# A graph network kernel on one Trainium2 core: gathers and scatters wait for the landing of the pair two back

## What is computed

```python
edge_index = jnp.stack([src, dst])
edge_index_t = jnp.stack([src, dst], axis=1)
h = jnp.maximum(_layernorm(x, axis=-1), 0.0)
x = x + _L0_gnn_ref(h, edge_attr_16, edge_index_t, ...)
h = jnp.maximum(_layernorm(x, axis=-1), 0.0)
x = x + _L1_gnn_ref(h, edge_index, edge_weight)

# _L0_gnn_ref: edge_index_t[:, 0] is the node that receives, edge_index_t[:, 1] the neighbour
edge_mats = (bond_features @ W_bond + b_bond).reshape(-1, d, d)
for _ in range(STEPS):                                    # STEPS = 4
    msg = jnp.einsum('eij,ej->ei', edge_mats, h[nbr])
    agg = jax.ops.segment_sum(msg, dst, num_segments=n_atoms)
    h = _gru_cell(agg, h, W_ih, W_hh, b_ih, b_hh)

# _L1_gnn_ref
msgs = x[row] * (deg_inv_sqrt[row] * edge_weight * deg_inv_sqrt[col])[:, None]
out = jax.ops.segment_sum(msgs, col, num_segments=num_nodes)
```

## Time and profile before

| | us |
|---|---|
| median of three runs | 32566.4 |
| lowest, highest | 32561.8, 32571.98 |
| the profiled execution | 32329.01 |
| its span, first to last instruction | 32327.5 |
| POOL busy in the span | 19193.7 (59%) |
| TensorE (PE) busy | 18113.4 (56%) |
| VectorE (DVE) busy | 12316.8 (38%) |
| ScalarE (ACT) busy | 6342.0 (20%) |

### The profile page before, as it was taken

One profiled execution on the slowest core, in us unless ns is written; L12 is line 12 of the kernel. 1 busy time (PEld: TensorE's weight loads), 2 busy tenths in 40 slices (PEclk: granted clock), 3 DMA queues, 4 the chain that ended last, 5 costly groups with the idle time before them and its releaser, 6 DMA issues. The chain is left out here.

```text
span 32327.5 us, 272049 instructions
## 1 busy us (share of the span) xinstructions
PE 18113.4 (56%) x73252; PEld 11303.4 (35%) x73253; DVE 12316.8 (38%) x18995; ACT 6342.0 (20%) x11838; POOL 19193.7 (59%) x19883
## 2 busy tenths in 40 slices
PE   5444444447777757777767777775777773000004
PEld 4222222224444434444434444443444442000003
DVE  7555555533333333333333333333333333111113
ACT  4222222212222212222212222221222221000000
POOL 2444444466666656666656666665666665777772
PEclk5666666678888878888878888887888886555555
DMA  2222222211111111111111111111111111222224
GB/s 87 81 77 77 81 77 77 81 35 29 29 29 29 29 25 29 29 29 28 29 26 27 29 29 29 30 28 25 29 29 30 30 29 36 55 55 55 55 55 123
DMA packets 2423090, 1449.76 MB, mean 45 GB/s; under 512 B 1772221, under 2 KB 2253002, under 8 KB 2404167
## 3 DMA queue, kind: packets, MB, share of 16 engines
q1 hardware_dynamic: 720484, 980.18, 10.0%
q0 software_dynamic: 635936, 335.84, 6.4%
q10 hardware_dynamic: 1066560, 132.51, 2.7%
HBM read 1035.83 MB, written 411.12 MB: 45 GB/s over the span
## 5 line engine op out<-in xcount | busy, mean ns | idle before, releaser
L1112 POOL DMA_INDIRECT h_rows<-h_table,rec x12928 | 12195.4, 943 | 7353.8 <-issue 3880.5
L1298 PE MATMUL outer<-a_masked,h_by_quarter 128*128 128x272 f32 x25856 | 8240.2, 447 | 5227.6 <-DVE h_by_quarter L1158 2359.8
L1298 PEld LDWEIGHTS outer<-a_masked,h_by_quarter 128*128 128x128 f32 x25856 | 5378.2, 216 | 9576.1 <-issue 7355.3
L1266 PE MATMUL msg_psum<-outer_sums,w_bond_blocks 128*128 128x512 f32 x13736 | 7718.0, 652 | 0.0
L1344 ACT COPY outer_sums<-outer 128x544 f32<-128x544 f32 x6464 | 3900.2, 613 | 15272.9 <-PE outer L1298 7098.1
L865 POOL DMA_INDIRECT edges_by_node<-row,place x3125 | 2992.3, 958 | 3188.2 <-DVE row L792 2273.2
L1598 POOL DMA_INDIRECT messages_by_bucket<-ms,ix x3232 | 3418.9, 1058 | 1149.1 <-issue 1124.9
L1150 DVE TENSOR_TENSOR a_masked<-rec,gates 128x4352 f32<-128x4352 f32 x808 | 3782.5, 4681 | 53.1 <-PE outer L1298 31.5
L1266 PEld LDWEIGHTS msg_psum<-outer_sums,w_bond_blocks 128*128 128x128 f32 x13736 | 2921.0, 213 | 923.6 <-issue 260.9
L1167 DVE TENSOR_TENSOR_SCAN scan<-carry_flags,scan,msg_psum 128x512 f32<-128x512 f32 x404 | 517.1, 1280 | 6706.2 <-PE msg_psum L1266 4495.5
L1158 DVE TENSOR_TENSOR h_by_quarter<-h_rows,gates 128x2048 f32<-128x2048 f32 x808 | 1846.0, 2285 | 1824.4 <-DMA h_rows<-h_table,rec 1786.2
(11 more groups left out here) (273 smaller groups left out, 12928.5 us busy)
## 6 DMA issues: line engine op xcount, KB each, us to landing
h_rows<-h_table,rec POOLq DMA_INDIRECT x12928
key_row<-source_keys SPq DMA_DIRECT2D x125, 1600.0 KB
rec<-edges_by_node SPq DMA_DIRECT2D x1010, 168.0 KB
carry_flags<-carry_flags SPq DMA_DIRECT2D x505, 256.0 KB
chunk_sums<-scan_t ACTq DMA_DIRECT2D x1616, 64.0 KB
low_key_row<-source_low_keys SPq DMA_DIRECT2D x126, 800.0 KB
mr<-messages_by_bucket SPq DMA_DIRECT2D x220, 392.0 KB, 3.0
messages_by_bucket<-zeros SPq DMA_DIRECT2D x125, 689.5 KB
```

Of the source, the lines that this page charges most:

```text
L1112: pool.indirect_dma_start(out=hb[r][:, u, :], out_offset=None, in_=ht, in_offset=bass.IndirectOffsetOnAxis(ap=rec[r][:, u, W_DST:W_DST + 1 ...
L1266: last = pe.matmul(pm[:, 0:GW], wb[:, k, :], ts[b][:, k, :], start=(k == 0), stop=(k == K1 - 1))
L1298: last = pe.matmul(pt[g % RING][:, u, 0:KC], hq[j][:, g * GPB + u, :, :].rearrange("p q d -> p (q d)"), am[j][:, g * GPB + u, :, :].rearra ...
```

## The change

POOL's transfers now wait for each other. The four semaphores `s_hg` no longer stand for the four buffers but for the pairs of gathers in turn: pair k of a tile (u = 2k and 2k+1) raises `s_hg[k % 4]`. Ahead of each pair stands a wait for the landing of the pair two back, also across tiles, with a `hold`; the first two pairs of a step's first tile are without it where nothing was issued yet. `spread_h` waits for all four semaphores in place of one.

The 25 scatters of an iteration are cut into eight turns (seven of three, one of four) over four semaphores `s_sc`, and each turn waits for the landing of the turn two back. A new semaphore `s_free` ("rows_free_again"), which POOL raises when it comes to an iteration's second turn, tells ScalarE and VectorE that the other `row` buffer may be written; they wait on it where they waited on `s_sc[b]`. The loop over iterations becomes `pairs_after_first`. No data transfer and no computation is added, taken out or made larger.

```diff
@@ the sort: semaphores
-            s_sc = [sem(f"rows_scattered{b}") for b in range(2)]
+            s_sc = [sem(f"rows_scattered{k}") for k in range(4)]
+            s_free = sem("rows_free_again")
+            TURNS = [(a, a + 3) for a in range(0, J1 - 4, 3)] + [(J1 - 4, J1)]
+            PER = [16 * sum(z - a for a, z in TURNS[k::4]) for k in range(4)]
@@ make_row (ScalarE) and place_stage 0 (VectorE)
-                        act.wait_ge(s_sc[b], i * (16 * J1))
+                        act.wait_ge(s_free, it + 1)
...
-                            dve.wait_ge(s_sc[b], i * (16 * J1))
+                            dve.wait_ge(s_free, it + 1)
@@ the scatters (POOL)
+                    pool.sem_inc(s_free, 2)
                     clear_flags(range(HB // 2))
-                    def scatter(it, b, i):
+                    def scatter(it, b, i, first):
                         pool.wait_ge(s_row, it + 3)
                         pool.wait_ge(s_place, it + 3)
                         hold(pool)
-                        for u in range(J1):
-                            pool.indirect_dma_start(
-                                out=r3, out_offset=bass.IndirectOffsetOnAxis(ap=place[b][:, u:u + 1], axis=0),
-                                in_=row[b][:, u, :], in_offset=None).then_inc(s_sc[b], 16)
-                    pairs(pool, IT1, scatter)
+                        for k, (u0, u1) in enumerate(TURNS):
+                            before = (k - 2) % 4
+                            after = 16 * sum(z - a for a, z in TURNS[before:max(0, k - 1):4])
+                            if not (first and k < 2):
+                                pool.wait_ge(s_sc[before], it * PER[before] + after)
+                                if k == 1:
+                                    pool.sem_inc(s_free, 1)
+                                else:
+                                    hold(pool)
+                            for u in range(u0, u1):
+                                pool.indirect_dma_start(
+                                    out=r3, out_offset=bass.IndirectOffsetOnAxis(ap=place[b][:, u:u + 1], axis=0),
+                                    in_=row[b][:, u, :], in_offset=None).then_inc(s_sc[k % 4], 16)
+                    pairs_after_first(pool, IT1, scatter)
@@ the steps: the gathers (POOL)
-            s_hg = [sem(f"h_gathered{j}") for j in range(RB)]
+            s_hg = [sem(f"h_gathered{k}") for k in range(4)]
+            HPI = 16 * J3 // 4
...
                                     if u in (0, LATER) and past:
                                         pool.wait_ge(s_t, n0 * NB + (j * NB + NB + (HALF // GPB if u else 0)))
                                         hold(pool)
+                                    k = u // 2
+                                    if u % 2 == 0 and (k >= 2 or j or past):
+                                        pool.wait_ge(s_hg[(k - 2) % 4], n0 * HPI + (j * HPI + 32 * ((k + 2) // 4)))
+                                        hold(pool)
                                     pool.indirect_dma_start(
                                         out=hb[r][:, u, :], out_offset=None, in_=ht,
                                         in_offset=bass.IndirectOffsetOnAxis(ap=rec[r][:, u, W_DST:W_DST + 1].bitcast(I32), axis=0)
-                                    ).then_inc(s_hg[r], 16)
+                                    ).then_inc(s_hg[k % 4], 16)
@@ the steps: spread_h (VectorE)
-                            dve.wait_ge(s_hg[r], (s * USES[b] + i) * (16 * J3) + 16 * J3)
+                            for landed in s_hg:
+                                dve.wait_ge(landed, n * HPI + HPI)
                             dve.wait_ge(s_t, n * NB + NB)
```

More of the change, by code:

```diff
@@ L124, in gnn_program @@
     assert T3 * P < BIG and T2 * P < BIG and HB <= P and HB * D <= 7 * 512 and NGR % 2 == 1 and NRUN % 4 == 0
-    assert RB == 2 * GI and GI * HT == TU and CT <= P and GW <= 512
+    assert J3 == 16 and RB == 2 * GI and GI * HT == TU and CT <= P and GW <= 512
     r3 = nc.dram_tensor("edges_by_node", [T3 * P, W3], F32).ap()
@@ L510, in gnn_program @@
             s_row = sem("rows_made")
-            s_sc = [sem(f"rows_scattered{b}") for b in range(2)]
+            s_sc = [sem(f"rows_scattered{k}") for k in range(4)]
+            s_free = sem("rows_free_again")
+            TURNS = [(a, a + 3) for a in range(0, J1 - 4, 3)] + [(J1 - 4, J1)]
+            PER = [16 * sum(z - a for a, z in TURNS[k::4]) for k in range(4)]
+            assert len(TURNS) == 8
             s_v3 = sem("place_chain")
@@ L863, in scatter @@
                         hold(pool)
-                        for u in range(J1):
-                            pool.indirect_dma_start(
-                                out=r3, out_offset=bass.IndirectOffsetOnAxis(ap=place[b][:, u:u + 1], axis=0),
-                                in_=row[b][:, u, :], in_offset=None).then_inc(s_sc[b], 16)
-                    pairs(pool, IT1, scatter)
-                    pool.wait_ge(s_sc[0], 16 * J1 * ((IT1 + 1) // 2))
-                    pool.wait_ge(s_sc[1], 16 * J1 * (IT1 // 2))
+                        for k, (u0, u1) in enumerate(TURNS):
[12 more added lines that the diff above has]
+                    pairs_after_first(pool, IT1, scatter)
+                    for k in range(4):
+                        pool.wait_ge(s_sc[k], PER[k] * IT1)
         lay = ExitStack()
```

## The result

| | before | after |
|---|---|---|
| median of four runs each, same chip, us | 32569.19 | 33981.29 |
| lowest, highest | 32561.8, 32580.95 | 33947.0, 34025.63 |
| span of the profiled execution | 32327.5 | 33970.1 |

The change makes the kernel 4.3% slower: the ratio is 1.0434, with an interval of 1.0416 to 1.0452. That is 1412 us where 133 were forecast, above the whole range. It is also above the rival in which the limit binds (33045 us).

The account below looks back on a forecast made before the run. The prediction took a ring of waits among POOL's gathers, spread_h and TensorE's outer to set the pace. Its terms, 10 + 36 + 87 = 133 us, on 32566.4 gave about 32700 us, 0.4% slower, range 32560 to 32960.

Parts of the forecast that it names:

- the limit binds: Rival, chance 0.12: in the steps one of the last two pairs stalls 0.94 us in 509 tiles; 478 us, 33045 us.
- What bounds the kernel: In a step no engine is full and a ring of waits sets the pace; POOL busy 3043 of 4890 us, TensorE 3606.
- The ring: In the steps POOL's gathers wait for outer (3.6 us each), spread_h for the gathers' landing, and outer for spread_h.
- Whether they are met at once: Steps, ahead of the gather pairs: landing waits met with 0.27 to 0.61 us to spare; 10 us, bounds nothing and 760.
- Waits that are met: Steps, ahead of some 6,460 pairs: waits and holds are covered by the gather's 0.94 us; costed at nothing.
- POOL's second wait at u = 10: Behind the old wait on s_t, POOL's restart passes one more instruction; 509 x 0.07 = 36 us, bounds nothing and 125.
- Four waits in `spread_h`: Two steps, 0.17 us, between the last landing and spread_h in 509 tiles; 87 us, bounds nothing and 194.
- The sort: POOL's turn waits fit into 18.3 us spare per iteration, s_free might come 0.51 us late; nothing taken, 64 us at most.
- The clock: TensorE in the steps: a longer stop can put one more group on the lower clock level; none taken, 69 us possible.
- My own tell-tale: Sign that the forecast is wrong: many stops of POOL inside a tile put down to a landing; no size given.

Follow-up runs that it names:

- spread_ahead: The kernel before with already met waits added ahead of spread_h, so that its landing wait stands two steps ahead of the operation; 0.9986 of before.
- before_free: The kernel before without POOL's two stops on s_t, ahead of u = 0 and u = 10; 1.2293 of before.
- steps_free: The limit of four gathers in the steps alone, without POOL's two stops on s_t; 1.2359 of the kernel before.
- the two under "Which tile": The limit in the steps alone, with four gathers under way in a group's first tile and eight in its second, 1.0127 of before; the other way round, 1.0435.

## Why the prediction was wrong

**What bounds the kernel** was half right. The ring is there, and POOL's stop at u = 10 is in it, but I read it as a wait that costs 3.6 us a time. The runs without it say that it is worth far more than it costs, and most of TensorE's late releases come there or at the stop ahead of u = 0 (940 of 1204 while u = 9 or u = 15 is POOL's last gather).

**The step that failed** is "Whether they are met at once", in two places. First, "the wait is met in time with 0.27 to 0.61 us to spare": both landings that I could see were those of a tile's last gathers, at quiet moments. In second tiles landings come later, as the 4.2 us above, and POOL stops 361 times inside a tile. The Trainium skill's DMA: Bandwidth & Descriptors, section "Anatomy of one DMA", with its fixed 2.0 us, agrees with neither: the rows show less at the quiet moments and twice as much here, and the measurements decide. Second, and this carried the size: "In the first ten gathers such a stall comes off the stop ahead of u = 10 ..., so that only one in the last pairs lengthens the ring". It does come off that stop, as forecast: stops there fall from 576 to 111. But the stop was not free time to be used up: taking it out alone costs 6.0%. With it gone, ten gathers run in a row up to u = 15 in the tile shown, most of TensorE's late releases come behind that row (830 of 1165), and POOL then waits at u = 0 for the late TensorE (its waits for `outer`, at u = 0 and u = 10 together, take 2707.5 us against 1851.5). The term that I set at 10 us, with a bound of 760, is about 1142 of the 1227 us of the steps: what is left when six may be under way, 85 us, is no more than the waits' own price.

**Waits that are met**: forecast 0, measured 85 to 213 us for all of them, those of `spread_h` included. **POOL's second wait at u = 10**, 36 us, was not measured apart and is within these. **Four waits in `spread_h`**: forecast 87 us, measured -45 us [-78, -13] by `spread_ahead`. The delay itself is there, and of the forecast size: where `spread_h` waits for the landing, it starts 1.66 us behind the last gather's end in that run, 1.64 in the kernel after and 1.48 before (medians). What failed is that it lengthens the step: 0.18 us in each of 551 tiles leave no trace in the time.

**The sort**: forecast 0, upper bound 64 us, measured 32 us alone [3, 65], and 30 us in its trace (first gather at 6822.5 against 6792.6). With both parts in, the stage is 96 us longer in the trace, but chips differ here: in six kernels with the sort untouched (`before_free`, `steps_free`, the two with the record loads cut, and the two under "Which tile") the first gather starts between 6830.9 and 6839.3 us, on a chip where before takes 32500 to 32511 us, and before takes 32569 on the chip of the kernel after. So how much of the 60 us more is the change's is open.

**The clock**: forecast 0, up to 69 us. TensorE is busy for 18617.6 us with the same 73,252 matmuls that took 18113.4, 504 us more; more of them ran on the lower level, and the granted clock of the whole execution is 0.747 in place of 0.759. The term was far too small, but it does not explain the loss by itself: without the stop at u = 10 TensorE was busy for 18108.5 us, no longer than before, and the kernel lost 6.0%.

**The rivals.** "The limit binds" named the mechanism's first half and its sign, but priced only stalls in the last pairs. My own tell-tale, "many stops of POOL inside a tile put down to a landing (the limit binds)", is what the trace shows.

**What is shown and what is not.** Shown: the steps' part alone makes 1.0379 of the 1.0434, in second tiles, with four under way and not with six; the stores of the sums and the loads of the records beside them don't matter to it; taking the stop at u = 10 away costs more than that without any limit. Not shown: what makes the landings late (the load of the flags was not cut), and that the lost stops are the whole of the change's loss, since no run kept both the limit and the stop. That the row of gathers itself holds up TensorE's releases is argued from the times at which they come: no run changed the gathers' rate, and by which path POOL's transfers could reach TensorE's semaphore, or its matmuls, stays open. It is also open whether the matmuls run late or only their raises of `s_t` come late, since their ends are modelled. No version beat the kernel before by more than 0.14%: the best, 0.9986, is `spread_h`'s landing wait two steps ahead.

## What to carry to other kernels

Before a wait is put down as slack that a new stall may use up, ask what else happens during it; take the wait out in a run of its own and see whether the time falls. A limit on transfers under way is safe only from the latest landing that the trace shows in any part of the loop, with the restart of the issuing engine added, and two more gathers (six in place of four) were worth 3.5% here. Where waits end by a "remote" release, compare the waiter's start with the modelled end of what releases it: here the sum of these differences grew with the loss, by about half to twice its size.

## What the runs showed of the hardware

- Without a stop on `s_t` in POOL's gathers the kernel takes 39962 us in place of 32511. ScalarE's copies then start up to 15.6 us behind the modelled end of their matmuls (and of the copy before); with the stop at u = 10 alone taken out, up to 13.0.
- Most such late releases come around the end of a row of gathers or behind it: in the median 2.65 us after u = 9 has ended in the kernel before and 2.03 us after u = 15 in the kernel after, most of them between 0 and 3 us.
- Where `spread_h` waited for the last gather of a tile (16 KB) in the kernel before, it started 1.48 us behind the end of that gather's issue (median of 509), so the gather had landed by then. In the tile shown of the kernel after, one landed 4.2 us behind it, beside loads of the flags and the records.
- A wait that is already met between two gathers costs at most 0.01 to 0.03 us, far under the 0.07 us that I had worked out for VectorE.
